# Experts' FFN in 32 steps of six or seven node tiles, seven picked columns per chunk, and results taken in front of the edge chunk

## The reference

```python
h = (x_flat @ W_gat).reshape(M, HEADS, NUM_EXPERTS)
e = leaky_relu(a_src[src] + a_dst[dst], 0.2)
ee = exp(e - segment_max(e, dst)[dst])
agg = segment_sum(h[src] * ee / denom[dst], dst) + b_gat
topk_s, topk_i = top_k(layernorm(agg) ... mean over heads, 2)
w = softmax(topk_s)
for ei in range(4):
    g = where(topk_i == ei, w, 0).sum(-1)
    hh = gelu(x @ W1[ei] + b1[ei])
    out = out + g[..., None] * (hh @ W2[ei] + b2[ei])
```

## Time and profile before

| | |
|---|---|
| median of 3 runs | 2942.56 us (2938.81 to 2943.4) |
| profiled execution | 2940.0 us, of which span 2937.9 us |
| mean granted TensorE clock | 0.733 |
| busy over the whole span | PE 51%, DVE 72%, ACT 41%, POOL 69% |
| the stage at issue | about 1656 to 2772 us of the span |
| after it | `carry` from 2775, `finish` from 2790 us |

### The profile page before, as it was taken

One profiled execution on the slowest core, in us unless ns is written; L12 is line 12 of the kernel. 1 busy time (PEld: TensorE's weight loads), 2 busy tenths in 40 slices (PEclk: granted clock), 3 DMA queues, 4 the chain that ended last, 5 costly groups with the idle time before them and its releaser, 6 DMA issues. The chain is left out here.

```text
span 2937.9 us, 21979 instructions
## 1 busy us (share of the span) xinstructions
PE 1496.6 (51%) x5476; PEld 949.3 (32%) x5476; DVE 2121.8 (72%) x3413; ACT 1206.4 (41%) x2381; POOL 2013.1 (69%) x1978
## 2 busy tenths in 40 slices
PE   2657730222212222222125179999899999984323
PEld 1433330111111111111025046555555555551122
DVE  6978889998888888888568255565655555657657
ACT  1532338776667776666334022222222232221012
POOL 0456457777777777777666677777777777777560
PEclk8878875555555555555555589999999999997666
DMA  4522547666666666666563312222222222222186
GB/s 137 186 68 68 148 126 238 229 225 214 209 204 216 219 218 207 218 218 213 190 176 105 107 30 49 49 67 51 49 49 49 49 53 53 61 50 44 17 304 230
DMA packets 222462, 395.96 MB, mean 135 GB/s; under 512 B 50867, under 2 KB 174370, under 8 KB 214912
## 3 DMA queue, kind: packets, MB, share of 16 engines
q1 hardware_dynamic: 137604, 263.49, 26.2%
q0 software_dynamic: 75632, 122.58, 18.0%
q10 hardware_dynamic: 9100, 8.50, 0.9%
HBM read 204.85 MB, written 189.59 MB: 134 GB/s over the span
## 5 line engine op out<-in xcount | busy, mean ns | idle before, releaser
L1234 POOL DMA_INDIRECT stage_got<-ffn_rows,setup_src_ffn x860 | 844.2, 982 | 261.8 <-issue 261.7
L1234 POOL DMA_INDIRECT edges_got<-gnn_rows,edges_src_gnn x728 | 756.4, 1039 | 241.7 <-issue 221.5
L1341 DVE TENSOR_TENSOR_SCAN stage_y<-stage_decays,stage_y 128x960 f32<-128x960 f32 (+2 forms) x256 | 520.7, 2088 | 5.1 <-issue 5.0
L2174 PE MATMUL stage_ph<-ffn_xt_all,stage_w 128*128 128x448 f32 x896 | 381.5, 566 | 102.0 <-ACT stage_hid L2235 40.3
L1357 ACT ACTIVATE stage_rows<-stage_y 128x3640 f32<-128x3640 f32 (+1 forms) x88 | 399.8, 4543 | 0.0
L1630 PE MATMUL stage_pm<-setup_ident,stage_mix_parts 128*128 128x128 f32 x98 | 33.4, 444 | 674.6 <-DVE stage_mix_parts L1703 602.3
L2296 DVE TENSOR_TENSOR stage_start_parts<-stage_pk,stage_of_tile 128x490 f32<-128x490 f32 x328 | 209.2, 667 | 115.8 <-PE stage_pk L2166 111.1
L2166 PE MATMUL stage_pk<-stage_start_parts 128*128 128x490 bf16 x984 | 244.3, 386 | 66.9 <-DVE stage_start_parts L2296 51.9
L1317 DVE TENSOR_TENSOR stage_y<-edges_got,stage_y 128x896 f32<-128x896 f32 x168 | 262.9, 1672 | 0.3 <-ACT stage_y L1299 0.3
L2174 PEld LDWEIGHTS stage_ph<-ffn_xt_all,stage_w 128*128 128x128 f32 x896 | 173.8, 197 | 243.9 <-issue 141.9
L1630 PEld LDWEIGHTS stage_pm<-setup_ident,stage_mix_parts 128*128 128x128 f32 x98 | 14.2, 204 | 705.0 <-DVE stage_mix_parts L1703 677.3
(11 more groups left out here) (481 smaller groups left out, 2903.3 us busy)
## 6 DMA issues: line engine op xcount, KB each, us to landing
state_gnn<-stage_rows SPq DMA_DIRECT2D x56, 1848.0 KB
y<-search_found SPq DMA_DIRECT2D x28, 896.0 KB, 4.2
tail_fin_y<-y SPq DMA_DIRECT2D x7, 3584.0 KB, 17.7
stage_got<-ffn_rows,setup_src_ffn POOLq DMA_INDIRECT x860
edges_got<-gnn_rows,edges_src_gnn POOLq DMA_INDIRECT x784, 3.6
state_ffn<-stage_rows SPq DMA_DIRECT2D x32, 384.0 KB, 2.4
mix_rows<-stage_mix_parts SPq DMA_DIRECT2D x49, 131.0 KB, 2.1
x_again_mix<-mix_rows SPq DMA_DIRECT2D x7, 917.0 KB, 6.1
```

The source lines that it names most:

```text
L1234: pool.indirect_dma_start(out=got[:, u, t, :], out_offset=None, in_=self.row_dram[g.name][:, :], in_offset=bass.IndirectOffsetOnAxis(ap=sr ...
L1341: ins = dve.tensor_tensor_scan(some, r[s][:, 0:b - a, :].rearrange("p c t -> p (c t)"), some, 0.0, ALU.mult, ALU.add)
L2174: mm = pe.matmul(ph[:, f % 2 * 2 + half, 0:HALF], w1[:, e, k, f * P:(f + 1) * P], xt_all[:, k, at(b * (B * P) + half * HALF, HALF)], start ...
```

## The change

Each expert's 49 tiles are now cut into eight pieces of 6, 6, 6, 6, 6, 6, 6 and 7 tiles, so there are 32 steps, one per chunk, 28 of six tiles (three pairs) and four of seven (four pairs). All chunks but the first pick 7 columns, so GpSimd gathers 32 + 31x25 = 807 columns and TensorE and VectorE pick 217 instead of 164. VectorE's step takes the results and picks first, then `choose(q+2)`, and `chunk(q)` comes last. ScalarE's step does `gelus(q+1)` first, then `factors(q)`, then `act_rows(q)`. SyncE stores a step's results before the chunk's rows.

```diff
-PICKED, PICKED_LATE = 5, 8
+PICKED = 7
...
-    return PICKED if c <= NT // FFN_BLOCK * EXPERTS else PICKED_LATE
+    return 0 if g is GNN or c == 0 else PICKED
...
+        each = FFN.chunks // EXPERTS
+        first_tile = [NT * n // each for n in range(each + 1)]
+        work = [(e, a, b - a) for e in range(EXPERTS) for a, b in zip(first_tile, first_tile[1:])]
+        steps = len(work)
+        pairs = [(n + 1) // 2 for e, a, n in work]
...
+            def of_pair(q, k):
+                n = picked(FFN, q + 1) if q + 1 < FFN.chunks else 0
+                return range(k * n // pairs[q], (k + 1) * n // pairs[q])
...
                 def step(q, s):
+                    e, a, n = work[q]
                     load_lanes(q + 2)
+                    sp.wait_ge(out_used, pairs_before(q + 1))
+                    sp.dma_start(by_tile[:, at(a, n), e, :], yrow[:, 0:n, :]).then_inc(y_out, 16)
                     edge.sp_store(sp, q, s)
-                    sp.wait_ge(out_used, q * BANKS + BANKS)
-                    sp.dma_start(by_tile[:, at(b * B, B), e, :], yrow[:, :, :]).then_inc(y_out, 16)
...
-                def step(b, e, q, s):
+                def step(q, s):
+                    if q + 1 < steps:
+                        gelus(q + 1, 1 - s)
                     factors(q, s)
-                    if q + 1 < steps:
-                        gelus((q + 1) // blocks, q + 1, 1 - s)
                     edge.act_rows(act, q, q // 2, s, s)
...
-                def step(b, e, q, s):
-                    chunk(q, q // 2, s)
+                def step(q, s):
                     if q > 0:
                         dve.wait_ge(y_out, q * 16)
-                    for k in range(BANKS):
-                        take(e, q, k)
-                        for j in of_pair(q + 1, k):
+                    for k in range(pairs[q]):
+                        take(q, k)
+                        for j in of_pair(q, k):
                             take_picked(q + 1, j)
                     dve.drain()
                     choose(q + 2)
+                    chunk(q, q // 2, s)
```

More of the change, by code:

```diff
@@ L2052, in ffn_and_experts @@
         B = FFN_BLOCK
[L2053 to L2057, removed]
+        each = FFN.chunks // EXPERTS
[3 more added lines that the diff above has]
+        pairs = [(n + 1) // 2 for e, a, n in work]
+        assert steps == FFN.chunks and max(n for e, a, n in work) == B
         with ExitStack() as here:
@@ L2066, in ffn_and_experts @@
             w_loaded, hid_made, hid_ready, out_made, out_used, room_free = (self.sem(here, n) for n in names)
-            R, T, MOST = FFN.row, FFN.chunk, max(PICKED, PICKED_LATE)
+            R, T, MOST = FFN.row, FFN.chunk, PICKED
             columns = picked_before(FFN.chunks)
@@ L2094, in walk, with pairs_before @@
                 for q in range(steps):
[L2095 to L2100, removed]
+                    step(q, q % 2)
+            def pairs_before(q):
+                return sum(pairs[0:q])
+            def of_pair(q, k):
+                n = picked(FFN, q + 1) if q + 1 < FFN.chunks else 0
+                return range(k * n // pairs[q], (k + 1) * n // pairs[q])
             @block.gpsimd
@@ L2133, in _ @@
                 load_lanes(1)
[L2135 removed]
+                def step(q, s):
+                    e, a, n = work[q]
                     load_lanes(q + 2)
+                    sp.wait_ge(out_used, pairs_before(q + 1))
+                    sp.dma_start(by_tile[:, at(a, n), e, :], yrow[:, 0:n, :]).then_inc(y_out, 16)
                     edge.sp_store(sp, q, s)
[L2138 to L2139 removed]
                 walk(step)
[L2141 to L2143 removed]
                 edge.sp_end(sp)
                 begun.sp_end(sp)
[L2146 removed]
+                sp.wait_ge(y_out, 16 * steps)
             @block.tensor
@@ L2168, in pick, with first_layer @@
                         mm.then_inc(pick_made, 1)
-                def first_layer(b, e, q, f, half):
+                def first_layer(q, f, half):
+                    e, a, n = work[q]
+                    cols = n * P // 2
                     if half == 0 and not (q == 0 and f < 2):
@@ L2178, in first_layer, with second_layer @@
                         mm.then_inc(hid_made, 1)
-                def second_layer(e, q, s, t):
-                    bank, side = t // 2 % 2, t % 2 * D
-                    pair = q * BANKS + t // 2
+                def second_layer(q, s, t):
+                    e, a, n = work[q]
+                    pair, side = pairs_before(q) + t // 2, t % 2 * D
+                    bank = pair % 2
                     if side == 0 and pair >= 2:
@@ L2187, in second_layer @@
                                        start=(f == 0), stop=(f == FT - 1))
-                    if side or t == B - 1:
+                    if side or t == n - 1:
                         mm.then_inc(out_made, 1)
-                def step(b, e, q, s):
-                    ahead = ((q + 1) % blocks, (q + 1) // blocks)
-                    more = q + 1 < steps
+                def step(q, s):
+                    more, n = q + 1 < steps, work[q][2]
                     pe.wait_ge(hid_ready, q * FT + FT)
[L2195 to L2198, removed]
+                    for h in range(4 if more else 0):
+                        first_layer(q + 1, h // 2, h % 2)
+                    for t in range(n):
+                        second_layer(q, s, t)
                         if more and 1 <= t < 5:
-                            first_layer(*ahead, q + 1, (t + 3) // 2, (t + 3) % 2)
-                        if t % 2 or t == B - 1:
-                            for j in of_pair(q + 1, t // 2):
+                            first_layer(q + 1, (t + 3) // 2, (t + 3) % 2)
+                        if t % 2 or t == n - 1:
+                            for j in of_pair(q, t // 2):
                                 pick(q + 1, j)
-                for n in range(FT * 2):
-                    if n == 4:
+                for h in range(FT * 2):
+                    if h == 4:
                         begun.pe_last(pe)
@@ L2208, in _ @@
                         pe.wait_ge(begun.done, 1)
-                    first_layer(0, 0, 0, n // 2, n % 2)
+                    first_layer(0, h // 2, h % 2)
                 walk(step)
-                for c in range(steps + 1, FFN.chunks):
-                    for j in range(picked(FFN, c)):
-                        pick(c, j)
             @block.scalar
@@ L2226, in factors, with gelus @@
                     edge.act_exps(act, c, s)
-                def gelus(e, q, s):
+                def gelus(q, s):
+                    e, a, n = work[q]
                     if q == 1:
@@ L2258, in places @@
                     by_chunk = self.edge_src["ffn"][:, :].rearrange("p (c t) -> p c t", t=T)
-                    for a, b in ((1, steps + 1), (steps + 1, FFN.chunks)):
+                    for a, b in ((1, FFN.chunks),):
                         n, col = picked(FFN, a), picked_before(a)
```

28 lines of the change are left out of this document (12 added, 16 removed).

## The result

The changed kernel takes 3119.38 us (median of 5 runs, 3116.15 to 3122.17), before 2939.25 us in the same runs: a ratio of 1.061, with a 95% interval of 1.0595 to 1.0626. It is 180 us slower. The forecast was slower, 3080 us, with a range up to 3110; the time lies 9 us above that range. The mechanism came as forecast; the sizes of two terms did not.

The account below looks back on a forecast made before the run. Gathers (33.75 us a chunk) bound the kernel, with a 31.3 us ring beneath. Thirty rings of 36.1 + 1.5 us plus 5 us put the last chunk 137 us later: 3080 us, range 3025 to 3110.

Parts of the forecast that it names:

- The ring through chunk, rows, table load, GELU and TensorE: Loop of waits from one VectorE chunk to the next, through ScalarE and TensorE; forecast 36.1 us, 31.3 before.
- leg A: From a chunk's start on VectorE to TensorE's restart after the GELU; forecast 9.3 us against 5.96 before.
- the stall: TensorE's wait for the GELU at the third hidden part; forecast nearly 5 us in each step.
- The start of chunk 0: When VectorE begins the first chunk, 35.4 us behind the start of step 0; forecast at 1756.5.
- The rival in which GpSimd stays the bound: GpSimd's gathers still set the pace: 66 us saved, 11 given back at the start, 2888 us; chance 0.09.
- the slow clock: TensorE at the 1.2 GHz level after its stall; forecast 1.5 us more in each step, from 0 to 1.8.
- the ring at full clock: Time from chunk to chunk in a step of six tiles without slow clock; forecast 36.1 us, bounds 34.4 to 37.2.
- The last chunk: When VectorE starts chunk 31; forecast at 2901.5, against 2764.66 before, 137 us later.
- steps of seven: Steps with a seventh tile on TensorE; forecast 1.7 us more each, three of the four within the thirty rings, 5 us.
- start and last step: Chunk 0 forecast at 1756.5; the last step, with no first layer and no picks, forecast at 12 us.
- the count for before: Same count for the old kernel, from TensorE's restart to the next chunk: 25.2 us against 25.3 measured; method therefore trusted.
- the upper bound: Slow end of the whole time, from a ring of 37.2 us plus 1.8 us slow clock: 3120 us, cut to 3110.

Follow-up runs that it names:

- e5: Changed kernel with ScalarE's GELUs of hidden parts 0 and 1 of step q+2 moved between exponentials and rows of chunk q; 2955.46 us, ratio 1.0052.
- e3: Changed kernel (32 steps, 7 picks) with the order of before on VectorE, ScalarE and SyncE; 2950.49 us, ratio 1.0025.
- e8: e3 with the 7 picks spread over the tiles on TensorE and VectorE instead of behind the pairs; 2884.63 us, ratio 0.9816.
- e2: Kernel before with 7 picks instead of 5 in chunks 1 to 28, nothing else; 2981.58 us, ratio 1.0121.
- e6: As e5, but the GELUs of parts 0 and 1 of step q+2 stand before the exponentials of chunk q too; 2927.48 us, ratio 0.9958.
- e7: e6 with the 7 picks spread over the tiles on TensorE and VectorE instead of behind the pairs; 2892.92 us, ratio 0.9843.
- e4: Changed kernel with 20 extra bf16 matmuls on TensorE in each step from step 1, where it stalls for the GELU; 3060.25 us, ratio 1.0387.
- e1: Kernel before with only the new order on VectorE, ScalarE and SyncE, steps and picks unchanged; 3038.69 us, ratio 1.0317.
- e9: Changed kernel in its own order, with only the picks spread over the tiles; 3011.24 us, ratio 1.0236.

## Why the forecast was right, and where not

**Right.** The gathers stop being the bound, and GpSimd waits about 7 us a chunk. The ring through chunk, rows, table load, GELU and TensorE takes their place: leg A, with scan and rows in front of the GELU, was forecast at 9.3 us and is 9.38; the stall was forecast at nearly 5 and is 4.79. e5 shows that the GELU's place behind scan and rows is the cause, and e3 that the order as a whole is. The start of chunk 0 was forecast at 1756.5 and is 1756.80. The rival in which GpSimd stays the bound is dead for this kernel, but it is e8's state: its 66 us, up to the last chunk, were there once the ring was under GpSimd's pace. One reading for that rival was wrong, without harm to the sum: by busy time TensorE leads in the earlier trace rows, 930 us (84% of the stage) against GpSimd's 844. The rule of the Trainium skill ("Perfetto Trace Analysis", Identifying the Most-Contended Engine) leaves TensorE's matmul time aside, and so it does name GpSimd, before (76%) and in the changed kernel (63%). Relieving GpSimd alone brings nothing here, though: with 53 or 56 gathers fewer, the changed kernel, e2 and e3 are none of them faster than before; e6 gains 13 us, and most of the gain comes with the picks spread (e7, e8).

**Wrong: the range, by two terms of the sum,** the slow clock (1.5 us per ring taken, 2.2 measured) and the ring at full clock (36.1 us taken, 36.8 measured). The last chunk was forecast at 2901.5 us and came at 2945.68, 44 us later; chunks were forecast 37 to 38 us apart and are 38.2 to 39.4, over 40 about the steps of seven. By the runs this is:

| term | forecast | measured | over 30 rings |
|---|---|---|---|
| slow clock per ring | 1.5 us | 2.2 us (e4, `choose` evened out) | 20 us |
| ring of six tiles, full clock | 36.1 us | 36.77 us | 20 us |
| steps of seven | 1.7 us each | 2.4 us (e4, the same) | 2 us |
| start and last step | 1756.5, 12 us | 1756.80, 14.03 us (12.43 in e4) | 2 us |

*The clock* was sized from four matmuls behind one stall (3.35 against 1.77 us). But the slow level also covers the picks behind them: 0.94 us lost on the quarter (2.34 against e4's 1.40) and 0.74 on the picks in the step shown. In steps of six the loss behind the restart is 1.4 to 2.6 us, about the steps of seven 2.5 to 2.8, where I had set 1.8 as the upper end. The trace of before could have told. Behind the slow quarter at 2473.47 in the earlier trace rows stand

```profile
2476.62 2.62 PE L2166 MATMUL stage_pk<-stage_start_parts 128*128 128x490 bf16 x6
2479.07 1.90 PE L2186 MATMUL stage_po<-stage_w,stage_hid 128*128 128x256 f32 x8
```

so from the restart to the tile 5.60 us pass; behind the quarter at 1763.13 it is 2.85, to this tile:

```profile
1765.98 1.89 PE L2186 MATMUL stage_po<-stage_w,stage_start_parts 128*128 128x256 f32 x8
```

That is 2.75 us lost and not 1.5; in the other slow restarts of before it is 1.6 to 1.7. The stretch to look at is from the restart to the first tile at full speed.

*The ring at full clock* was 0.67 short. Leg A is 0.08 of it. A pair with two picks takes TensorE 2.80 us and not 2 x 1.24 (0.3 each for two pairs, of which I had 0.3 in all), the first quarter behind the restart takes 1.40 and not 1.29, and `choose` takes 0.95 us (2108.89 to 2109.84), not 0.8, a cost that I had seen and set to nothing. e2 shows the same fault larger: two picks cost 4.6 us where I took 2.8. That the count for before came out at 25.2 for 25.3 proved little, as before had only one place with two picks together.

Each error is small; 30 rings multiply it. My range cut the upper bound (3120, which would have held the time; by its own terms it is 3122) to 3110 with no measurement behind the cut.

**e7 beside e8.** With the GELUs moved (e7) TensorE never stalls for a GELU after the start, and still the kernel is 8 us above the old order with the same picks (e8). Its chunk 0 starts 40 us later, and the gathers of chunk 2 wait for it, GpSimd's only wait of that kind in the stage:

```profile
1756.38 2.11 POOL L1232 DMA_INDIRECT stage_got<-ffn_rows,setup_src_ffn  x1 [16.60 <-DVE stage_y L1307]
```

Later GpSimd sets the pace, as in e8; its last gather and the last chunk (2712.77) come 14 us later than there. Behind it e7 has 173 us and e8 182, which gives back 9. No run moved chunk 0 alone to test this.

**Open:** why the slow clock's loss differs from step to step, and why restarts behind stalls of much the same length are slow in one step and fast in another.

## What to carry to other kernels

When the engine that sets the pace is relieved, look for the ring that stands just under it: here 31.3 us against 33.75, seen only in the few steps in which the gathers were ahead. An in-order engine couples what its code puts side by side: a scan and two row copies in front of a GELU cost 164 us with the clock that fell in the longer stall. Where one engine takes twice as long over a unit of work as the engine that feeds it, spread the units; it was worth 66 us at no cost in work.

## What the runs showed of the hardware

A stall of 3.5 to 4.8 us of TensorE in every step costs 1.4 to 2.8 us more in slow clock behind nearly every one, with a pattern that repeats every two or three steps (lost from restart to tile, e1: 2.7; the changed kernel: 2.6, 1.7, 1.4; e9: 2.5, 1.6). Stalls of 1.6 us (e3, e5) cost nothing. The length alone does not settle it: in the kernel before, three stalls of 3.3 to 3.4 us, from the one at 2542.27 in the earlier trace rows on, cost nothing, and one of 1.97 us, at 1925.75, cost 1.7. Filling the stall with 20 matmuls whose result nobody reads made the kernel 59 us faster. GpSimd's first gather after a wait for VectorE took 2.1 to 2.2 us instead of 0.94 in 29 of the changed kernel's 30 waits. VectorE's scan runs beside it; in the kernel before the gather at 1761.93, beside a scan, took 1.46. What makes up the rest is not shown.
